# Self-attention's row-maximum product: 64 rows a head instead of 128, two heads on the two row halves of TensorE's array

## The chip, the cores and the metric

The kernel runs on one core of a Trainium2 chip. The metric is the device time of one execution in microseconds (us), the median of several runs. TensorE (PE) multiplies, VectorE (DVE), ScalarE (ACT) and GpSimd (POOL) do the element-wise work, SyncE (SP) issues the DMAs.

## What is computed

One transformer block on x (2 x 1024 rows of 256) with a context of 2 x 154 rows of 192: layer norm, self-attention, layer norm, cross-attention, layer norm, gated feed-forward, each with a residual. The part that matters here is attention with 16 heads of 64:

```python
q = (xq @ wq).reshape(B, S, N_HEADS, D_HEAD)
k = (xkv @ wk).reshape(B, T, N_HEADS, D_HEAD)
v = (xkv @ wv).reshape(B, T, N_HEADS, D_HEAD)
scale = D_HEAD ** (-0.5)
attn = jnp.einsum('bihd,bjhd->bhij', q, k) * scale
attn = jax.nn.softmax(attn, axis=-1)
out = jnp.einsum('bhij,bjhd->bihd', attn, v).reshape(B, S, D_ATTN)
return out @ wo + bo
```

## The kernel before, in words

Activations lie transposed in SBUF (features on partitions). A float32 operand of a product is held as a high half that TensorE's fp32r format keeps exactly (written by ACT) and a low half, the rest (a subtraction on DVE or POOL); a projection is then three products, high x high, high x low, low x high.

Attention goes over `NPAIR` = 16 pairs of heads (8 pairs for each of the 2 sequences), J = 0 to 15. Each engine has an order written out by hand, `SELF_ORDER` and `CROSS_ORDER` (L61, L76), which `bodies` (L151) emits once per pair as one body: words with "-" belong to pair J-1, without a sign to J, with "+" to J+1, with "++" to J+2. So a body of self-attention holds the softmax products of one pair beside the preparation of the next. The words, with PE's work for each:

- K, Q, V (two halves of 512 columns each): the projections, 6 matmuls of 512 columns at L502 each.
- T: four transposes of values (L529). M: the transpose of the row maxima (L556).
- X0 to X31: the product for the row maximum (L546). One matmul takes 128 queries against 512 keys of one head; DVE then takes its maximum over the 512 keys (`tensor_reduce`, L767). Before the change a query's operand `qq[b][:, h, ...]` holds 128 rows for each head: its 64 high halves on the head's own partitions (0-63 for head 0 of the pair, 64-127 for head 1) and its 64 low halves on the other ones; `kk` holds the high halves of the keys on both (the second copy is ACT's, semaphore `k_twice`).
- S u.h: the scores of 128 keys against 512 queries for head h, two matmuls (L569, L570), the second of which also subtracts the row maximum; ACT takes the exponential (L950).
- P u: probabilities times values, one matmul for each of the two heads, into 64 output columns each (L582), in float32: the trace has two MATMUL records for each. D: the sums of the exponentials, of the same form (L591), followed by a reciprocal on DVE (L784).
- Y half.m: the output projection, three matmuls (L606 to L608) into bank `FOLD`, then an addition on DVE (L794).

What ties the engines around X: two PSUM banks take the X products in turn (`mx_banks` = 2). X number n waits until DVE has read number n-2 (`x_read`, "`after(pe, S["x_read"], n - plan.mx_banks + 1)`"). DVE works its own order strictly one after the other, and that order is not changed:

```python
"dve": "R0- K0+ D1- K1+ Q0+ X0+ X1+ X2+ Q1+ X3+ X4+ X5+ X6+ X7+ X8+ X9+ X10+ Y0.0- X11+ X12+ X13+ R1- "
       "X14+ Y0.1- X15+ X16+ C0+ X17+ X18+ X19+ X20+ X21+ X22+ X23+ X24+ X25+ X26+ X27+ X28+ M0+ D0 "
       "X29+ X30+ Y1.0- X31+ C1+ M1+ Y1.1-",
```

There K and Q are the two subtractions that give the low halves (L761), R the multiplication by the reciprocal (L789), C a small maximum (L775), M a copy (L780).

On TensorE a matmul whose operands lie on 128 partitions and that gives 128 columns uses the whole array, which is called whole-array here; P and D use half the columns each and are called column-half here.

Of the kernel before, what the change touches and what calls it, by code (L numbers as in the profile page):

```python
# [30 lines left out]
HEADS, DH = 16, 64  # L31
# [3 lines left out]
P = 128  # L35
KD = DM // P
KC, PC = 2, DC // 2
HALF = 512
# [21 lines left out]

SELF_ORDER = {  # L61
# [102 lines left out]
def block_kernel(nc, io, out):  # L164
    with ExitStack() as ctx:
# [157 lines left out]
        def prep_use(plan, kind, a, J, b):  # L323


            use = plan.at[kind] + a
            which = (plan.nprep * b + use) % plan.prep_banks
            g = plan.nprep * J + use
            return g, PREP - which, sems[plan][f"prep_free{which}"], g if plan.prep_banks == 1 else g // 2
# [82 lines left out]
        def _(pe):  # L412
            def bank(n, width=HALF):
                return psum[:, n, 0:width]
# [75 lines left out]
            def attention(plan, h_count):  # L490
                S = sems[plan]
# [13 lines left out]
                def emit(steps, par):  # L505
                    for kind, J, a, dp in steps:
# [24 lines left out]
                            mm.then_inc(S["prep_ready"], 1)  # L531
                        elif kind == "X":
                            n = plan.tiles * J + a
                            if a == 0:
                                pe.wait_ge(S["k_twice"], plan.khalf * (J + 1))
                            if a in (0, plan.tiles // 2):
                                if plan is CROSS:
                                    pe.wait_ge(S["q_lo"], 4 * J + 2 + 2 * (a // (plan.tiles // 2)))
                                else:
                                    _, _, split, reads = prep_use(plan, "Q", a // (plan.tiles // 2), J, b)  # L540
                                    pe.wait_ge(split, reads + 1)
                            after(pe, S["x_read"], n - plan.mx_banks + 1)
                            if plan.khalf == 2:
                                half, h, t, kh = a // 16, a // 2 % 2, a // 4 % 4, a % 2
                                q0 = half * HALF + t * P
                                mm = pe.matmul(bank(PV + plan.pv_banks + a % plan.mx_banks), qq[b][:, h, q0:q0 + P], kk[b][:, h, kh * HALF:(kh + 1) * HALF],  # L546
                                               start=True, stop=True)
                            else:
                                for h in range(2):
                                    mm = pe.matmul(psum[:, PV + plan.pv_banks + a % plan.mx_banks, h * plan.keys:(h + 1) * plan.keys],  # L550
                                                   qq[b][:, h, a * P:(a + 1) * P], kk[b][:, h, 0:plan.keys], start=True, stop=True)
# [129 lines left out]
        def _(dve):  # L681
# [62 lines left out]
            def attention(plan, h_count):  # L744
# [3 lines left out]
                def emit(steps, par):  # L748
                    for kind, J, a, dp in steps:
# [13 lines left out]
                        elif kind == "X":  # L763
                            dve.wait_ge(S["x_ready"], plan.tiles * J + a + 1)
                            if plan.khalf == 2:
                                half, h, t, kh = a // 16, a // 2 % 2, a // 4 % 4, a % 2
                                dve.tensor_reduce(m_part[:, half, h, t, kh:kh + 1], psum[:, PV + plan.pv_banks + a % plan.mx_banks, :], AX.X,  # L767
                                                  ALU.max).then_inc(S["x_read"], 1)
                            else:
# [371 lines left out]
```

## Time and profile before

| | |
|---|---|
| runs of the kernel before | 1566.72, 1568.81, 1576.96 us |
| median | 1568.81 us |
| span of the profiled execution | 1578.7 us |
| PE busy | 1469.8 us (93%) |
| DVE busy | 979.5 us (62%) |
| mean granted TensorE clock | 0.958 of full speed |

The page gives the profiled execution's span and no separate time for it; it lies 9.9 us (0.6%) above the median of the runs. Self-attention fills the stretch from about 60 to 930 us. How to read the views: a busy time counts the records' own durations, and those of matmuls are modelled and overlap each other, so the pace of PE is read from the starts of successive matmuls. "PEld" is the load of the weights (the stationary operand) that goes before each matmul.

### The profile page before, as it was taken

The page shows a single profiled execution, that of the slowest core. Times are in us where ns is not written, and L with a number is a line of the kernel's source. Part 1 is how long each engine was busy: PE and PEld are TensorE (multiplying, and loading weights), DVE is VectorE, ACT ScalarE, POOL GpSimd, SP SyncE. Part 2 cuts the span into 40 slices and gives each one's busy share as a digit, 9 for nine tenths or more (in the row PEclk, how much of TensorE's full clock was granted, in tenths as well). Part 3 has the DMA queues.
Part 4 walks back from the last instruction along what each step waited for, and adds up shares of the span by engine and source line. Part 5 has one row for each costly group of instructions (what it writes and reads, how often), then busy time and mean ns, then how long its engine had stood idle before and what let it go on. Part 6 is the DMA issues. An engine that isn't in the chain of part 4 may idle for free.

```text
span 1578.7 us, 21167 instructions
## 1 busy us (share of the span) xinstructions
PE 1469.8 (93%) x5921; PEld 821.4 (52%) x5921; DVE 979.5 (62%) x1311; ACT 858.7 (54%) x1498; POOL 923.3 (58%) x513
## 2 busy tenths in 40 slices
PE   5589999999999999999999998689999999968998
PEld 3344555555555555555555543344555555426776
DVE  6457766766776676677667643536777777744333
ACT  4346565565655656565565643546666667535333
POOL 6026767757766775776677687436667777553000
PEclk9689999999999999999999998869999999979999
DMA  2000000000000000000000000200000000000000
GB/s 70 11 14 14 13 2 14 15 0 13 13 1 13 13 13 0 13 13 0 13 14 3 1 13 0 88 20 18 24 24 24 12 24 24 7 1 0 14 13 27
DMA packets 35737, 24.07 MB, mean 15 GB/s; under 512 B 2845, under 2 KB 35443, under 8 KB 35443
## 3 DMA queue, kind: packets, MB, share of 16 engines
q1 hardware_dynamic: 35699, 23.60, 4.9%
q8 instruction: 20, 0.33, 0.1%
q14 instruction: 18, 0.15, 0.0%
HBM read 21.23 MB, written 2.10 MB: 15 GB/s over the span
## 4 chain that ended last, share of the span: by engine, by line
PE 83%; ACT 6%; DVE 5%; POOL 3%; issue 2%; DMA 0%; ACTq 0%; SPq 0%; DVEq 0%; POOLq 0%
PE psum L582 20%; PE psum L502 13%; PE psum L569 11%; PE psum L546 9%; PE psum L570 8%; PE psum L655 5%; PE psum L591 4%; PE psum L644 3%; PE psum L606 2%; PE psum L608 2%; PE psum L607 2%; ACT probs L950 2%; PE psum L550 1%; PE psum L443 1%; PE psum L529 1%
## 5 line engine op out<-in xcount | busy, mean ns | idle before, releaser
L1083 POOL TENSOR_TENSOR acc<-acc,probs 128x1024 f32<-128x1024 f32 x192 | 458.2, 2386 | 184.3 <-ACT probs L950 175.1
L950 ACT ACTIVATE probs<-psum 128x512 f32<-128x512 f32 (+1 forms) x640 | 368.1, 594 | 256.9 <-PE psum L570 234.5
L767 DVE TENSOR_REDUCE m_part<-psum 128x1 f32<-128x512 f32 x512 | 344.9, 687 | 113.0 <-PE psum L546 108.7
L582 PE MATMUL psum<-probs,val 128*64 128x512 f32 (+1 forms) x1280 | 340.8, 620 | 0.2 <-ACT probs L950 0.2
L784 DVE RECIPROCAL recip<-psum 128x512 f32<-128x512 f32 x64 | 214.9, 3358 | 79.0 <-PE psum L591 79.0
L1083 POOL TENSOR_TENSOR acc<-probs 128x1024 f32<-128x1024 f32 (+1 forms) x64 | 152.7, 2386 | 120.1 <-ACT probs L950 71.0
L569 PE MATMUL psum<-qq,self_keys_hh 128*128 128x512 f32 x512 | 219.3, 428 | 2.2 <-ACT probs L950 2.1
L546 PE MATMUL psum<-self_keys_hh,qq 128*128 128x512 f32 x512 | 210.5, 431 | 6.1 <-DVE qq L761 2.8
L570 PE MATMUL psum<-qm,self_keys_lm 128*128 128x512 f32 x512 | 202.9, 396 | 0.0
L569 PEld LDWEIGHTS psum<-qq,self_keys_hh 128*128 128x128 f32 x512 | 96.7, 189 | 121.5 <-ACT probs L950 56.6
L546 PEld LDWEIGHTS psum<-self_keys_hh,qq 128*128 128x128 f32 x512 | 96.1, 190 | 117.5 <-DVE m_part L767 60.6
L502 PE MATMUL psum<-h_hi,w_hi 128*128 (+1 forms) x256 | 112.2, 438 | 21.9 <-POOL w_lo L1049 12.1
L1092 POOL TENSOR_TENSOR qq<-q_full,qq 64x512 fp32r<-64x512 f32 x64 | 81.8, 1278 | 83.4 <-ACT q_full L924 80.8
L582 PEld LDWEIGHTS psum<-probs,val 128*64 128x64 f32 (+1 forms) x1280 | 67.0, 136 | 116.9 <-issue 100.4
L794 DVE TENSOR_TENSOR xT<-xT,psum 128x512 f32 (+1 forms) x128 | 87.5, 684 | 57.6 <-PE psum L608 56.0
L1097 POOL TENSOR_TENSOR o_lo<-oT,o_hi 128x512 fp32r<-128x512 f32 x64 | 82.1, 1283 | 60.3 <-ACT o_hi L955 59.2
L502 PE MATMUL psum<-h_hi,w_lo 128*128 (+1 forms) x256 | 106.1, 414 | 0.0
L502 PE MATMUL psum<-h_lo,w_hi 128*128 (+1 forms) x256 | 105.7, 413 | 0.0
L570 PEld LDWEIGHTS psum<-qm,self_keys_lm 128*128 128x128 f32 x512 | 97.0, 189 | 13.6
L920 ACT ACTIVATE qq<-psum 64x512 fp32r<-64x512 f32 x128 | 75.6, 590 | 39.7 <-PE psum L502 38.3
L770 DVE TENSOR_REDUCE m_part<-psum 128x2 f32<-128x308 f32 x128 | 60.8, 475 | 56.1 <-PE psum L550 56.1
L955 ACT ACTIVATE o_hi<-oT 128x512 fp32r<-128x512 f32 x64 | 40.4, 632 | 93.7 <-DVE oT L789 55.6
(122 smaller groups left out, 2165.5 us busy)
## 6 DMA issues: line engine op xcount, KB each, us to landing
w_raw<-in_L_xattn_ff_w SPq DMA_DIRECT2D x3, 1024.0 KB, 6.8
x_in<-in_x SPq DMA_DIRECT2D x4, 512.0 KB, 4.2
w_raw<-in_L_xattn_sa_wq SPq DMA_DIRECT2D x16, 128.0 KB, 2.1
w_raw<-in_L_xattn_sa_wk SPq DMA_DIRECT2D x16, 128.0 KB, 2.3
w_raw<-in_L_xattn_sa_wv SPq DMA_DIRECT2D x16, 128.0 KB, 2.4
qm<-m_rows SPq DMA_DIRECT2D x128, 2.0 KB
wo_raw<-in_L_xattn_sa_wo SPq DMA_DIRECT2D x16, 128.0 KB, 2.1
w_raw<-in_L_xattn_ca_wq SPq DMA_DIRECT2D x16, 128.0 KB, 2.3
```

The source lines that it names most:

```text
L502: mm = pe.matmul(bank(prep, n), w, x, start=(k == 0 and m == 0), stop=(k == kin - 1 and m == 2))
L546: mm = pe.matmul(bank(PV + plan.pv_banks + a % plan.mx_banks), qq[b][:, h, q0:q0 + P], kk[b][:, h, kh * HALF:(kh + 1) * HALF], start=True, ...
L569: pe.matmul(psum[0:plan.ks, SC + h, :], kk[b][:, h, ks], qq[b][:, h, qs], start=True, stop=False)
L570: pe.matmul(psum[0:plan.ks, SC + h, :], kl[b][:, h, ks], qm[b][:, h, qs], start=False, stop=True).then_inc(S["s_ready"], 1)
L582: mm = pe.matmul(psum[d, PV + half % plan.pv_banks, :], val[b][0:plan.ks, kt, d], probs[a % 4][0:plan.ks, h, :], start=(kt == 0), stop=(kt ...
L767: dve.tensor_reduce(m_part[:, half, h, t, kh:kh + 1], psum[:, PV + plan.pv_banks + a % plan.mx_banks, :], AX.X, ALU.max).then_inc(S["x_rea ...
L784: dve.reciprocal(recip[:], psum[:, FOLD, :]).then_inc(S["sums_read"], 1)
L794: dve.tensor_tensor(x, x, psum[:, FOLD, :], ALU.add).then_inc(S["y_added"], 1)
L950: act.activation(probs[u % 4][0:plan.ks, h, :], psum[0:plan.ks, SC + h, :], ACT.Exp, scale=SCALE).then_inc(S["exp_done"], 1)
L1083: pool.tensor_tensor(total, last if kt == 1 else total, now, ALU.add).then_inc(S["acc_done"], 1)
L1092: pool.tensor_tensor(qq[b][other, h, half], q_full[own, a, :], qq[b][own, h, half], ALU.subtract).then_inc(S["q_lo"], 1)
L1097: pool.tensor_tensor(o_lo[:], oT[:], o_hi[:], ALU.subtract).then_inc(S["o_lo"], 1)
```

## The change

For self-attention alone the product for the row maximum contracts 64 rows, the high halves of one head on that head's own partitions, in place of 128. So the low halves of the queries no longer enter the row maximum (it is subtracted from the scores and divides out again). The index of a product is turned so that an even X and the odd one after it are head 0 and head 1 of the same queries and keys: the first lies on partitions 0-63, the second on 64-127, and they write two banks. X0 and X16 no longer wait for the second copy of the keys (`k_twice`) and for the low halves of the queries, but for their high halves (`hi_ready`). PE's order is rewritten so that the 32 X stand in 16 pairs; the order of DVE, ACT, POOL and SP stays. All lines from L541 on move down by one (L546 is L547 in the changed kernel, L582 is L583).

```diff
@@ SELF_ORDER
-    "pe": "S0.0 S0.1 K0+ P13- S1.0 P14- S1.1 D1- K1+ S2.0 S2.1 P15- P0 P1 S3.0 Q0+ S3.1 S4.0 P2 S4.1 S5.0 "
-          "X0+ Q1+ X1+ S5.1 X2+ S6.0 Y0.0- X3+ P3 X4+ V0+ X5+ X6+ P4 V1+ X7+ X8+ P5 X9+ S6.1 X10+ S7.0 "
-          "X11+ P6 X12+ T0+ X13+ S7.1 X14+ S8.0 Y0.1- S8.1 X15+ X16+ P7 X17+ S9.0 X18+ T1+ X19+ S9.1 X20+ "
-          "S10.0 X21+ S10.1 X22+ S11.0 X23+ P8 X24+ X25+ P9 X26+ S11.1 X27+ S12.0 X28+ M0+ S12.1 D0 S13.0 "
-          "S13.1 P10 X29+ P11 S14.0 X30+ S14.1 Y1.0- X31+ P12 S15.0 S15.1 Y1.1- M1+",
+    "pe": "S0.0 S0.1 K0+ P13- S1.0 P14- S1.1 D1- K1+ S2.0 S2.1 P15- P0 P1 S3.0 Q0+ S3.1 S4.0 P2 S4.1 S5.0 X0+ "
+          "X1+ Q1+ S5.1 X2+ X3+ S6.0 Y0.0- P3 X4+ X5+ V0+ X6+ X7+ P4 V1+ X8+ X9+ P5 S6.1 X10+ X11+ S7.0 P6 "
+          "X12+ X13+ T0+ S7.1 X14+ X15+ S8.0 Y0.1- S8.1 X16+ X17+ P7 S9.0 X18+ X19+ T1+ S9.1 X20+ X21+ S10.0 "
+          "S10.1 X22+ X23+ S11.0 P8 X24+ X25+ P9 X26+ X27+ S11.1 S12.0 X28+ X29+ M0+ S12.1 D0 S13.0 S13.1 P10 "
+          "P11 S14.0 X30+ X31+ S14.1 Y1.0- P12 S15.0 S15.1 Y1.1- M1+",
@@ PE, kind "X"
-                            if a == 0:
+                            if a == 0 and plan is CROSS:
                                 pe.wait_ge(S["k_twice"], plan.khalf * (J + 1))
                             if a in (0, plan.tiles // 2):
+                                second = a // (plan.tiles // 2)
                                 if plan is CROSS:
-                                    pe.wait_ge(S["q_lo"], 4 * J + 2 + 2 * (a // (plan.tiles // 2)))
+                                    pe.wait_ge(S["q_lo"], 4 * J + 2 + 2 * second)
                                 else:
-                                    _, _, split, reads = prep_use(plan, "Q", a // (plan.tiles // 2), J, b)
-                                    pe.wait_ge(split, reads + 1)
+                                    pe.wait_ge(S["hi_ready"], plan.nsplit * J + plan.khalf + second + 1)
                             after(pe, S["x_read"], n - plan.mx_banks + 1)
                             if plan.khalf == 2:
-                                half, h, t, kh = a // 16, a // 2 % 2, a // 4 % 4, a % 2
+                                half, t, kh, h = a // 16, a // 4 % 4, a // 2 % 2, a % 2
                                 q0 = half * HALF + t * P
-                                mm = pe.matmul(bank(PV + plan.pv_banks + a % plan.mx_banks), qq[b][:, h, q0:q0 + P], kk[b][:, h, kh * HALF:(kh + 1) * HALF],
-                                               start=True, stop=True)
+                                own = slice(h * DH, (h + 1) * DH)
+                                mm = pe.matmul(bank(PV + plan.pv_banks + a % plan.mx_banks), qq[b][own, h, q0:q0 + P],
+                                               kk[b][own, h, kh * HALF:(kh + 1) * HALF], start=True, stop=True)
@@ DVE, kind "X"
-                                half, h, t, kh = a // 16, a // 2 % 2, a // 4 % 4, a % 2
+                                half, t, kh, h = a // 16, a // 4 % 4, a // 2 % 2, a % 2
```

On PE, from X14 to the product P7 behind it (L546 and L547 are X, L569/L570 and L570/L571 are S, L606 to L608 and L607 to L609 are Y0.1, L582 is P). Before:

```order
L546 MATMUL psum<-self_keys_hh,qq 128x512 [waits self_x_read]
L569 MATMUL psum<-qq,self_keys_hh 128x512 [waits self_exp_done,self_m_moved1,self_q_again]
L570 MATMUL psum<-qm,self_keys_lm 128x512
L606 MATMUL psum<-o_hi,wo_hi 128x512 [waits self_y_added]
L607 MATMUL psum<-o_lo,wo_hi 128x512
L608 MATMUL psum<-o_hi,wo_lo 128x512
L569 MATMUL psum<-qq,self_keys_hh 128x512 [waits self_exp_done]
L570 MATMUL psum<-qm,self_keys_lm 128x512
L546 MATMUL psum<-self_keys_hh,qq 128x512 [waits self_x_read]
L546 MATMUL psum<-self_keys_hh,qq 128x512 [waits self_x_read,self_prep_free0]
L582 MATMUL psum<-probs,val 64x512 [waits self_exp_done]
```

The same place in the changed kernel:

```order
L547 MATMUL psum<-self_keys_hh,qq 128x512 [waits self_x_read] x2
L570 MATMUL psum<-qq,self_keys_hh 128x512 [waits self_exp_done,self_m_moved1,self_q_again]
L571 MATMUL psum<-qm,self_keys_lm 128x512
L607 MATMUL psum<-o_hi,wo_hi 128x512 [waits self_y_added]
L608 MATMUL psum<-o_lo,wo_hi 128x512
L609 MATMUL psum<-o_hi,wo_lo 128x512
L570 MATMUL psum<-qq,self_keys_hh 128x512 [waits self_exp_done]
L571 MATMUL psum<-qm,self_keys_lm 128x512
L547 MATMUL psum<-self_keys_hh,qq 128x512 [waits self_x_read,self_hi_ready]
L547 MATMUL psum<-self_keys_hh,qq 128x512 [waits self_x_read]
L583 MATMUL psum<-probs,val 64x512 [waits self_exp_done]
```

X15 has moved from behind Y0.1 to a place ahead of S8.0, beside X14; X17 has moved ahead of P7, beside X16.

The second place is PE around T1 (L529) and the scores that follow it. Before:

```order
L546 MATMUL psum<-self_keys_hh,qq 128x512 [waits self_x_read]
L529 MATMUL psum<-ident,valT 128x128 [waits self_prep_free0]
L529 MATMUL psum<-ident,valT 128x128 x3
L546 MATMUL psum<-self_keys_hh,qq 128x512 [waits self_x_read]
L569 MATMUL psum<-qq,self_keys_hh 128x512 [waits self_exp_done]
L570 MATMUL psum<-qm,self_keys_lm 128x512
L546 MATMUL psum<-self_keys_hh,qq 128x512 [waits self_x_read]
```

The same place in the changed kernel:

```order
L547 MATMUL psum<-self_keys_hh,qq 128x512 [waits self_x_read] x2
L529 MATMUL psum<-ident,valT 128x128 [waits self_prep_free0]
L529 MATMUL psum<-ident,valT 128x128 x3
L570 MATMUL psum<-qq,self_keys_hh 128x512 [waits self_exp_done]
L571 MATMUL psum<-qm,self_keys_lm 128x512
L547 MATMUL psum<-self_keys_hh,qq 128x512 [waits self_x_read] x2
```

X19 has moved ahead of T1, and X20 and X21 stand together behind S9.1.

## Rows read from the trace of the kernel before

**Rows 1.** The page: busy time of the engines, then the chain that ended last.
```profile
PE 1469.8 (93%) x5921; PEld 821.4 (52%) x5921; DVE 979.5 (62%) x1311; ACT 858.7 (54%) x1498; POOL 923.3 (58%) x513
...
PE 83%; ACT 6%; DVE 5%; POOL 3%; issue 2%; DMA 0%; ACTq 0%; SPq 0%; DVEq 0%; POOLq 0%
```

**Rows 2.** Stretch: its us; busy us PE, PEld, DVE, ACT, POOL; PEclk; DMA share, GB/s.
```profile
442.70:885.00 442.30, 442.30 (x1799) 240.62 (x1799) 302.24 (x414) 257.69 (x444) 304.56 (x144) 1.00 0.03 9
60.00:110.00 50.00, 42.03 (x116) 24.04 (x117) 27.83 (x46) 20.66 (x34) 8.43 (x4) 0.79 0.04 11
```

**Rows 3.** PE's waits from 110 to 900 us: all there are.
```profile
PE psum L569 <- ACT probs L950: 0.3, 1, 0.3
```

**Rows 4.** PE's timeline: start us, us, engine, line, operation, count.
```profile
501.02 0.39 PE L546 MATMUL psum<-self_keys_hh,qq 128*128 128x512 f32 x1
501.33 1.08 PE L582 MATMUL psum<-probs,val 128*64 128x512 f32 x4
502.34 0.50 PE L546 MATMUL psum<-self_keys_hh,qq 128*128 128x512 f32 x1
502.68 0.40 PE L502 MATMUL psum<-h_hi,w_hi 128*128 x1
502.92 0.39 PE L502 MATMUL psum<-h_lo,w_hi 128*128 x1
```

**Rows 5.** PE's timeline around three P that follow each other, and the page's group.
```profile
545.14 2.79 PE L582 MATMUL psum<-probs,val 128*64 128x512 f32 x12
547.87 0.50 PE L569 MATMUL psum<-qq,self_keys_hh 128*128 128x512 f32 x1
...
L582 PE MATMUL psum<-probs,val 128*64 128x512 f32 (+1 forms) x1280 | 340.8, 620 | 0.2 <-ACT probs L950 0.2
```

**Rows 6.** Timeline of weight loads around the one product on few rows (34).
```profile
9.41 0.19 PEld L443 LDWEIGHTS psum<-xT,mean_w 128*128 128x128 f32 x1 [0.34 <-issue]
10.36 0.14 PEld L428 LDWEIGHTS psum<-ident,vec_rows 34*128 34x128 f32 x1 [0.76 <-issue]
10.54 0.31 PEld L423 LDWEIGHTS psum<-ident,x_in 128*128 128x128 f32 x3
```

**Rows 7.** DVE's timeline: reads of X (L767) and what stands between them.
```profile
500.77 1.39 DVE L761 TENSOR_TENSOR qq<-psum,qq 64x512 fp32r<-64x512 f32 x2
502.19 1.38 DVE L767 TENSOR_REDUCE m_part<-psum 128x1 f32<-128x512 f32 x2
504.51 1.29 DVE L767 TENSOR_REDUCE m_part<-psum 128x1 f32<-128x512 f32 x2 [0.94 <-PE psum L546]
...
510.69 0.69 DVE L794 TENSOR_TENSOR xT<-xT,psum 128x512 f32 x1
511.29 2.17 DVE L767 TENSOR_REDUCE m_part<-psum 128x1 f32<-128x512 f32 x3
...
514.73 0.69 DVE L794 TENSOR_TENSOR xT<-xT,psum 128x512 f32 x1
515.33 1.28 DVE L767 TENSOR_REDUCE m_part<-psum 128x1 f32<-128x512 f32 x2
...
527.25 3.36 DVE L784 RECIPROCAL recip<-psum 128x512 f32<-128x512 f32 x1 [0.72 <-PE psum L591]
```

**Rows 8.** PE's timeline at the products that those DVE rows follow.
```profile
504.08 0.40 PE L546 MATMUL psum<-self_keys_hh,qq 128*128 128x512 f32 x1
...
511.90 0.60 PE L529 MATMUL psum<-ident,valT 128*128 128x128 f32 x4
...
512.57 0.39 PE L569 MATMUL psum<-qq,self_keys_hh 128*128 128x512 f32 x1
...
514.18 0.39 PE L608 MATMUL psum<-o_hi,wo_lo 128*128 128x512 f32 x1
...
526.12 1.08 PE L591 MATMUL psum<-acc,ones 128*64 128x512 f32 x4
```

**Rows 9.** PE's waits from 60 to 110 us.
```profile
PE psum L546 <- DVE qq L761: 2.8, 1, 2.8
```

## The prediction

> **What bounds the kernel now.** I read the page first: PE is busy for 93% of the span, no other engine for more than 62%, and the chain that ended last lies on PE for 83% [rows 1]. Then the stretches: from 442.7 to 885 us PE is busy for all of the 442.3 us at a granted clock of 1.00 (its level of 2.4 GHz), and DVE for 302 us of them [rows 2]. Last the waits: from 110 to 900 us PE waited 0.3 us in all [rows 3]. So in self-attention, outside its start, PE runs from one instruction into the next. Two things follow: what shortens PE's own stream is gained in full, and any wait that is new on PE is lost in full. DVE has slack on average, but it reads X products in a fixed order between other work.
>
> **How PE spends its time.** A whole-array matmul of 512 columns starts 0.23 to 0.24 us after the one before it [rows 4]; I take 0.233. P is a change of shape: three P in a row last from 545.14 to 547.87, 2.73 us, one alone from 501.33 to 502.34, 1.01 us, so each further P costs 0.86 and 0.15 is paid once [rows 4, 5]. The start of P comes 0.31 after the whole-array matmul ahead of it, 0.08 to 0.10 late, and the second whole-array matmul behind P 0.34 after the first, 0.11 late [rows 4]. I read that as a pause of 0.10 at each change of shape, and behind it a weight load that lies in the open: 0.05 for 64 columns, 0.11 for 128. In the pure stream the load is hidden under the matmul before. That prices an entrance into P at 0.15 and one into a shape with 128 columns at 0.21.
>
> Is the new product, 64 rows by 128 columns, a change of shape too? There is one near case, a product on 34 rows. The load ahead of the whole-array stream there is 0.76 us idle with no releaser, starts at 10.36 after that stream has finished and does not run ahead beneath it, and so does the load of the next whole-array product at 10.54 [rows 6]. I take it as a change of shape, both ways.
>
> The Trainium skill says the same against this change: by "TensorEngine Tiling (Array Packing)", Key Properties, another tiling mode, though not another tile of one mode, drains TensorE. By the same page's table of theoretical speedup a contraction of 64 rows or less gains up to 2x. Which wins is what the sum below decides; by the second sentence alone the X would be worth half their time, and that is the fourth rival.
>
> **The X products themselves.** 32 X of 0.233 are 7.46 us in a body. If the two of a pair run side by side, as the two heads of P do (1280 records of 620 ns would be 794 us, and P is busy for 340.8 [rows 5]), 16 pairs of 0.22 are 3.52. Saved: 3.94.
>
> **The changes of shape.** Counted in the two orders of PE. Before, a body has 16 column-half stretches (P15 P0 P1 together, D0 and D1 among them), with 16 entrances to whole-array. After, P10 and P11 stand together, so 15; the 16 pairs of X are stretches of their own; 8 borders lie directly between a pair and a P (at P3, P4, P5, P6, P7, two sides of X24 X25, and P9 to X26), which leaves 15 + 16 - 8 = 23 returns to whole-array. Added: 16 entrances into row halves at 0.21, 3.36; 7 more returns at 0.21, 1.47; one entrance into P less, -0.15. Together 4.68. Against the 3.94 saved the stream itself is 0.74 us longer in a body.
>
> The bounds of this unseen price: if it is nothing, the stream is 3.94 + 0.35 (the excursion into P that the joining of P10 and P11 saves) = 4.3 shorter. If the pairs do not run side by side at all, each costs a further 0.22, 3.5 in a body. I take the middle value, the price of P, the row it is nearest to.
>
> **The new waits.** X n waits for the read of X n-2. Singles left time for that; now the second of a pair needs the second of the pair ahead. DVE starts 0.44 after the X starts (504.08, 504.51), a second read comes 0.60 later, each lasts 0.69 [rows 7, 8]. A pair that starts at 0 is read until 0.44 + 0.60 + 0.69 = 1.73. Then the load in the open, 0.11, and about 0.05 for the semaphore: the next pair's second product can't start before 1.89. On PE the next pair starts at 0.22 + 0.21 + work between + 0.21, with S = 0.46, Y = 0.69, P = 0.86, and T = 0.67 - 0.23 = 0.44 (511.90 to 512.57 less one X) [rows 8]. Where a P lies between, an entrance of 0.15 and a further 0.21 come in. Most gaps suffice. Six do not:
>
> X3 to X5: DVE has Q1's two subtractions before X3 (from 500.77 to 502.19, 1.42 [rows 7]), so X3 is read until 0.44 + 0.72 + 1.42 + 0.69 = 3.27, restart at 3.43; PE comes after 0.22 + 0.21 + S + Y + 0.15 + P + 0.21 = 2.80. Wait 0.63.
>
> X11 to X13: DVE adds Y0.0 before X11 (0.60, 510.69 to 511.29), restart at 2.49; PE comes at 0.22 + 0.21 + S + 0.15 + P + 0.21 = 2.11. Wait 0.38.
>
> X15 to X17: DVE adds Y0.1 before X15, and Y0.1 now comes after X15 on PE, not before. Its last matmul starts 0.22 + 0.21 + 2 x 0.46 = 1.35 after the pair, the addition 0.55 later (514.18, 514.73), the read 0.60 later, 0.69 long: 3.19, restart 3.35. PE comes at 0.43 + S + Y + S + 0.21 = 2.25. Wait 1.10, the largest.
>
> X19 to X21, across T1 and one S: 1.54 against 1.89. Wait 0.35. X25 to X27, across P9: 1.44 against 1.89. Wait 0.45.
>
> X29 to X31: X29 stands behind D0's reciprocal on DVE. D0 starts on PE 1.02 after the pair (0.43, M 0.03, S, a pause of 0.10), the reciprocal 1.13 later (526.12, 527.25), 3.36 long, the read 0.69: 6.20, restart 6.36. PE, by way of D0, two S, P10, P11 and one S, comes at 5.83. Wait 0.53.
>
> The gaps across two S (X22, X28) come to 1.56, but there the pair ahead started its first product early by its own wait, so the reads have ended in time. The six are 3.44 us in a body. Nothing behind PE covers this: it had no waits to give back [rows 3].
>
> **What costs nothing.** The turned index changes only which maximum goes where. The waits of X0 and X16 for `k_twice` and the low halves go; PE waited once, 2.8 us, for the latter, at the start [rows 9], but DVE makes those low halves before it reads X0 in its unchanged order, so the read is no earlier. The later reads of X31 and X15 feed C1 and C0, with several P and S between them and M.
>
> **The sum.** 0.74 + 3.44 = 4.2 us in a body, in the 15 bodies that prepare a next pair beside softmax work; the first pair's X lie in the opening stretch, where PE is busy for 42 of 50 us and goes by DVE's reads [rows 2], and change nothing. 15 x 4.2 = 63 us. On the profiled execution's span of 1578.7 that is 1642, on the median of the runs, 9.9 lower, 1568.8 + 63 = 1632. From no change 1% can be told, 16 us. I forecast 1632, with 1605 to 1660 if the mechanism holds (a quarter off in the waits is 13 us, 0.05 off in the 22 added borders 16).
>
> **Rivals.**
> Pairs one after the other: the second product has a wait of its own, which P's second has not, and that may keep it apart. Then 16 x 0.22 more, less what hides in the six waits (6 x 0.22): 2.2 x 15 = 33, 1665. Against it: P's heads overlap as the busy time says [rows 5]. Chance 0.10.
>
> Borders cost nothing, waits as above: for it only that the 34-row case is one row. The stream is 4.3 shorter, but the gaps shrink with it: the six waits grow by 0.2 to 0.4 each, to some 5.1. 0.8 x 15 = 12, 1581. Chance 0.15.
>
> Borders cost as with P, but the waits are hidden, because reads come earlier than my rows say: 0.74 x 15 = 11, 1580. Chance 0.06.
>
> Faster: borders cost nothing and DVE keeps pace with half the waits gone (2.5 a body): 4.3 - 2.5 = 1.8 x 15 = 27, 1542, and with all of them gone 1504. It is decided where the waits in a body stay under the 4.3 us that the stream saves. For it: DVE's load is 68% in this stretch; against it: the read of a pair takes 1.29, and the order puts an addition and a reciprocal inside a pair. Chance 0.11.
>
> **How the numbers follow.** The forecast holds 0.58, the slower rival 0.10, the two near no change 0.21, the faster one 0.11. The two near no change lie just inside 1% (to 1584.5), but some of their spread falls outside: same 0.17, faster 0.12, slower 0.71. The range runs from 1572, which takes in the two, to 1668, which takes in the serial pairs; the faster case is left out.
>
> **What would show it.** In the changed trace: L547 records in pairs with starts a few ns apart; the load of the next whole-array product 0.1 after them and not beneath them; PE waiting for DVE's L768 six times in a body, longest ahead of X17; PE's busy share in the stretch below 100%; a body longer by some 4 us. Wrong would be: pairs of 0.22 between whole-array products at the plain pace (then the border price falls), starts 0.22 apart (then they are serial), or PE's waits for L768 under 1 us in a body.

## The result and the profile after

| | before | after |
|---|---|---|
| median of 4 runs each | 1570.01 us | 1643.30 us |
| all runs | 1566.72 to 1576.96 | 1641.12 to 1644.03 |
| span of the profiled execution | 1578.7 | 1641.7 |

The ratio is 1.0447, with a 95% interval from 1.0409 to 1.0484: slower by 4.5%. (Here and below the ratio is an estimate from the single runs, so it is not exactly the quotient of the medians beside it.) Forecast were 1632 us in a range from 1572 to 1668. By the spans of the two profiled executions the change costs 63.0 us, by the medians 73. The other ten I put down to a stretch behind self-attention, in which the granted clock of one and the same kernel differs from run to run (last section).

The page of the changed kernel. PE is as busy by share as in [rows 1], and DVE, which was 5% of the chain, is 7%:

```profile
PE 1522.3 (93%) x5921; PEld 787.3 (48%) x5921; DVE 970.4 (59%) x1311; ACT 855.9 (52%) x1498; POOL 922.9 (56%) x513
...
PE 81%; DVE 7%; ACT 6%; issue 3%; POOL 3%; DMA 0%; ACTq 0%; SPq 0%; DVEq 0%; POOLq 0%
...
L547 PE MATMUL psum<-self_keys_hh,qq 64*128 64x512 f32 x512 | 178.3, 511 | 18.0 <-DVE m_part L768 14.9
```

The same stretch as in [rows 2] (columns as there) has fallen from 100% busy to 98.9%, and does fewer matmuls, 1682 for 1799. That is 6.5% less work, of which the busy share shows 1.1 points:

```profile
442.70:885.00 442.30, 437.25 (x1682) 208.05 (x1680) 276.54 (x380) 240.80 (x419) 283.20 (x134) 1.00 0.03 10
```

**A pair between whole-array products.** PE's timeline of the changed kernel (start us, us, engine, line, operation, count). L571 is the second half of an S, L570 the first of the next:

```profile
541.02 0.40 PE L571 MATMUL psum<-qm,self_keys_lm 128*128 128x512 f32 x1
541.35 0.49 PE L547 MATMUL psum<-self_keys_hh,qq 64*128 64x512 f32 x2
541.78 0.50 PE L570 MATMUL psum<-qq,self_keys_hh 128*128 128x512 f32 x1
542.11 0.40 PE L571 MATMUL psum<-qm,self_keys_lm 128*128 128x512 f32 x1
542.44 1.08 PE L583 MATMUL psum<-probs,val 128*64 128x512 f32 x4
```

The two products of a pair are merged in one row of 0.49 us, no longer than one of them: they run side by side, as the change intends. But the row starts 0.33 after the one before (0.23 is the plain pace), the next whole-array product starts 0.43 after it, and the one after that 0.33 later again. From 541.02 to 542.11 are 1.09 us for a pair and two starts of the plain pace (0.47): the pair costs 0.62. Two whole-array X cost 0.47. So the product itself is halved, and still the pair costs 0.15 more than the two products that it replaces. The forecast had 0.64 for it (0.21 + 0.22 + 0.21).

The weight loads show where that goes. Within a whole-array stretch the record of a load starts 0.23 us ahead of its matmul (the median), beneath the matmul before. From 200 to 880 us of the changed kernel there are 613 changes of shape of all kinds, 89 of them between X and P, and at every one the load starts within 3 ns of its matmul: none runs ahead.

**A pair held back.** The same view at X16, X17, behind Y0.1 (L607 to L609):

```profile
546.90 0.40 PE L609 MATMUL psum<-o_hi,wo_lo 128*128 128x512 f32 x1
547.13 0.40 PE L570 MATMUL psum<-qq,self_keys_hh 128*128 128x512 f32 x1
547.37 0.40 PE L571 MATMUL psum<-qm,self_keys_lm 128*128 128x512 f32 x1
547.70 0.49 PE L547 MATMUL psum<-self_keys_hh,qq 64*128 64x512 f32 x1
548.79 0.50 PE L547 MATMUL psum<-self_keys_hh,qq 64*128 64x512 f32 x1 [0.60 <-DVE m_part L768]
```

and DVE at that time (L768 reads an X, L795 adds a Y):

```profile
545.97 0.69 DVE L768 TENSOR_REDUCE m_part<-psum 128x1 f32<-128x512 f32 x1
547.45 0.69 DVE L795 TENSOR_TENSOR xT<-xT,psum 128x512 f32 x1 [0.79 <-PE psum L609]
548.06 1.28 DVE L768 TENSOR_REDUCE m_part<-psum 128x1 f32<-128x512 f32 x2
```

X14 is read at 545.97. X15, its partner, is in its bank as well, but stands behind the addition of Y0.1 in DVE's order; DVE sits idle for 0.79 us until PE has made Y0.1, adds, and reads X15 from 548.06 to 548.75. X17 starts at 548.79. It comes 1.09 us after X16, where the forecast had 1.10. The row says "0.60" idle: the record of X16 is modelled to last until 548.19, so a wait on PE is read from the starts, not from the idle column. The list of PE's waits, which had a single line in [rows 3], shows only 8.6 us from 110 to 950 us for the same reason:

```profile
PE psum L547 <- DVE m_part L768: 8.6, 14, 0.8
```

From the starts, the second product of a pair comes late at six places in every steady body, and at no other: 0.61 at X5, 0.50 at X13, 1.10 at X17, 0.38 at X21, 0.43 at X27, 0.42 at X31 (medians over the 15 bodies), 3.44 us in all. In the other ten pairs it starts within 10 ns of the first.

**The length of a body.** The steady part repeats so evenly that one number carries most comparisons below: the time from the first X of one body to that of the next, taken as the mean over 13 bodies (J = 2 to J = 15, counted from 0). Before it is 55.66 us (X0 of J = 2 at 163.2, of J = 15 at 886.9), after 59.62 (170.6, 945.7). The difference is 3.96.

### The profile page after: what moved, and what is told of

It is laid out like the page before. It is cut to its first block, busy times and chain, and to the rows that moved or that the text cites. A ratio compares the mean times of both kernels' runs of the same rounds, so it can differ in the third digit from the quotient of the medians.

```text
span 1641.7 us, 21178 instructions
## 1 busy us (share of the span) xinstructions
PE 1522.3 (93%) x5921; PEld 787.3 (48%) x5921; DVE 970.4 (59%) x1311; ACT 855.9 (52%) x1498; POOL 922.9 (56%) x513
## 4 chain that ended last, share of the span: by engine, by line
PE 81%; DVE 7%; ACT 6%; issue 3%; POOL 3%; DMA 0%; ACTq 0%; SPq 0%; DVEq 0%; POOLq 0%
PE psum L583 18%; PE psum L502 13%; PE psum L570 11%; PE psum L547 9%; PE psum L571 8%; PE psum L656 5%; PE psum L592 4%; PE psum L645 2%; PE psum L607 2%; DVE m_part L768 2%; ACT probs L951 2%; PE psum L609 2%; PE psum L608 2%; DVE qq L762 1%; PE psum L529 1%
## 5 line engine op out<-in xcount | busy, mean ns | idle before, releaser
L768 DVE TENSOR_REDUCE m_part<-psum 128x1 f32<-128x512 f32 x512 | 335.8, 686 | 167.3 <-PE psum L547 163.4
L583 PE MATMUL psum<-probs,val 128*64 128x512 f32 (+1 forms) x1280 | 337.4, 619 | 0.2 <-ACT probs L951 0.2
L570 PE MATMUL psum<-qq,self_keys_hh 128*128 128x512 f32 x512 | 235.9, 461 | 2.3 <-ACT probs L951 2.3
L571 PE MATMUL psum<-qm,self_keys_lm 128*128 128x512 f32 x512 | 203.1, 397 | 0.0
L547 PE MATMUL psum<-self_keys_hh,qq 64*128 64x512 f32 x512 | 178.3, 511 | 18.0 <-DVE m_part L768 14.9
L570 PEld LDWEIGHTS psum<-qq,self_keys_hh 128*128 128x128 f32 x512 | 97.2, 190 | 162.2 <-issue 77.7
L547 PEld LDWEIGHTS psum<-self_keys_hh,qq 64*128 64x128 f32 x512 | 67.6, 188 | 167.8 <-DVE m_part L768 113.2
L502 PE MATMUL psum<-h_hi,w_hi 128*128 (+1 forms) x256 | 115.6, 452 | 20.3 <-POOL w_lo L1050 10.9
L795 DVE TENSOR_TENSOR xT<-xT,psum 128x512 f32 (+1 forms) x128 | 87.6, 684 | 76.1 <-PE psum L609 75.6
L583 PEld LDWEIGHTS psum<-probs,val 128*64 128x64 f32 (+1 forms) x1280 | 68.2, 136 | 114.7 <-issue 91.4
L571 PEld LDWEIGHTS psum<-qm,self_keys_lm 128*128 128x128 f32 x512 | 97.4, 190 | 7.8
```

The lines of the kernel that those rows point to most:

```text
L502: mm = pe.matmul(bank(prep, n), w, x, start=(k == 0 and m == 0), stop=(k == kin - 1 and m == 2))
L570: pe.matmul(psum[0:plan.ks, SC + h, :], kk[b][:, h, ks], qq[b][:, h, qs], start=True, stop=False)
L571: pe.matmul(psum[0:plan.ks, SC + h, :], kl[b][:, h, ks], qm[b][:, h, qs], start=False, stop=True).then_inc(S["s_ready"], 1)
L583: mm = pe.matmul(psum[d, PV + half % plan.pv_banks, :], val[b][0:plan.ks, kt, d], probs[a % 4][0:plan.ks, h, :], start=(kt == 0), stop=(kt ...
L795: dve.tensor_tensor(x, x, psum[:, FOLD, :], ALU.add).then_inc(S["y_added"], 1)
```

## The experiments

Ten kernels ran. In the times below "before" stands for the kernel before on the same chip and in the same session; its median was 1579.64 (e1 to e4), 1577.99 (e5 to e8) and 1577.48 us (e9, e10), with single runs from 1566.45 to 1581.04. Body lengths come from each kernel's own trace.

| kernel | median us | ratio to before (95%) | body us |
|---|---|---|---|
| before | 1570.01 | | 55.66 |
| after | 1643.30 | 1.0447 (1.0409 to 1.0484) | 59.62 |
| e1 order only | 1614.17 | 1.0227 (1.0161 to 1.0292) | 58.05 |
| e2 rows only | 1680.51 | 1.0668 (1.0607 to 1.0730) | 62.33 |
| e3 spaced | 1593.28 | 1.0086 (1.0056 to 1.0117) | 56.50 |
| e4 joined | 1596.45 | 1.0107 (1.0042 to 1.0173) | 56.71 |
| e5 one exchange on DVE | 1616.05 | 1.0239 (1.0222 to 1.0256) | 58.53 |
| e6 old waits of X0, X16 | 1636.19 | 1.0361 (1.0338 to 1.0384) | 59.62 |
| e7 both on one half | 1659.69 | 1.0506 (1.0465 to 1.0548) | 61.10 |
| e8 joined, second try | 1554.41 | 0.9861 (0.9835 to 0.9888) | 54.36 |
| e9 64 rows beside P only | 1557.27 | 0.9869 (0.9830 to 0.9909) | 54.22 |
| e10 joined, one more | 1551.95 | 0.9850 (0.9816 to 0.9883) | 54.15 |

**e1, the order alone.** The changed kernel with these edits:

```diff
-                            if a == 0 and plan is CROSS:
+                            if a == 0:
...
-                                    pe.wait_ge(S["hi_ready"], plan.nsplit * J + plan.khalf + second + 1)
+                                    _, _, split, reads = prep_use(plan, "Q", second, J, b)
+                                    pe.wait_ge(split, reads + 1)
...
-                                mm = pe.matmul(..., qq[b][own, h, q0:q0 + P], kk[b][own, h, ...])
+                                mm = pe.matmul(..., qq[b][:, h, q0:q0 + P], kk[b][:, h, ...])
```

> The changed order of TensorE with the old product on 128 rows and the old waits of X0 and X16 (the index with two heads side by side stays). Leaves out nothing. Theory (the change costs by borders between shapes and by waits for reads, each about half): the borders fall to 15 into and 15 out of the column-half shape, 0.36 us a body fewer than before; the waits stay, but each gap is 0.25 us longer because an X pair takes 0.47 in place of 0.22: about 2.8 us a body, the largest ahead of X17. Net 2.4 x 15 = 37 us over before, about 1607. Rival 1 (only the 64-row shape costs): 1565, no wait of TensorE for the reads. Rival 2 (only the order costs): 1643.

Measured: 1614.17 us, a body of 58.05, 2.39 over before where 2.4 was expected. PE waits in the trace, longest ahead of X17 again (the second X comes 1.20 after the first, where 0.23 is plain). So with the product on 128 rows untouched, pairing it in the order costs 36 us by bodies (15 x 2.39), 34.5 by medians. Rival 1 falls, and so does rival 2: the order by itself costs a good half of what the change costs, and not all of it.

**e2, the shape alone.** The changed kernel with the "pe" line of the kernel before.

> The 64-row product, two heads by turns, in the old order of TensorE, where most X stand alone. Theory: 28 stretches in the row-half shape in each body, each with an entrance and a return; 28 x 0.21 + 12 x 0.21 = 8.4 us a body of borders more than before, 0.4 saved where two X stand together and by the plain length, no new waits for reads: 8.0 x 15 = 120 us over before, about 1690. Rival 1 (a border costs nothing, only the order's waits do): 1570. Rival 2 (borders at half the price): 1630.

Measured: 1680.51 us, 101 above before; a body of 62.33, 6.67 longer, where 8.0 was expected. The only wait of PE that the list shows from 110 to 900 us is the 0.3 us of [rows 3], the starts show no late X either, and in the stretch PE is busy throughout:

```profile
442.70:885.00 442.30, 442.30 (x1603) 204.17 (x1602) 271.38 (x372) 229.70 (x397) 270.18 (x128) 1.00 0.03 8
```

So the borders alone, with no wait at all, cost more than the whole change. That a border is free falls; at half price the time would have been 1630. The expectation took too little for what the new product saves: X5 X6, X7 X8, X15 X16 and X24 X25 start within 10 ns of each other here too, so 28 stretches of 0.22 stand in place of 32 products of 0.233, which saves 1.3 in a body and not 0.4. Forty borders were added in a body, 28 entrances and 12 returns: (6.67 + 1.3) / 40 is 0.20 for each, close to the 0.21.

e1 and e2 don't add up to the change (2.39 + 6.67 against 3.96), because pairing does two things: it makes the waits, and it cuts the added borders from 40 to 22 and lets all the products run two at a time.

**e3, the waits taken out.** The changed kernel with these orders (ACT, POOL and SP as before):

```diff
-          "... S7.1 X14+ X15+ S8.0 Y0.1- S8.1 X16+ X17+ P7 S9.0 X18+ X19+ T1+ S9.1 X20+ X21+ S10.0 "
-          "S10.1 X22+ X23+ S11.0 P8 X24+ X25+ P9 X26+ X27+ S11.1 S12.0 X28+ X29+ M0+ S12.1 D0 S13.0 S13.1 P10 "
-          "P11 S14.0 X30+ X31+ S14.1 Y1.0- P12 ..."
+          "... S7.1 S8.0 X14+ X15+ Y0.1- S8.1 X16+ X17+ P7 S9.0 X18+ X19+ T1+ S9.1 S10.0 X20+ X21+ "
+          "S10.1 S11.0 X22+ X23+ P8 S11.1 X24+ X25+ P9 S12.0 X26+ X27+ M0+ S12.1 D0 X28+ X29+ S13.0 S13.1 "
+          "P10 P11 S14.0 S14.1 Y1.0- X30+ X31+ P12 ..."
-    "dve": "... X2+ Q1+ X3+ X4+ X5+ X6+ ... X10+ Y0.0- X11+ ... X14+ Y0.1- X15+ ... X28+ M0+ D0 X29+ X30+ Y1.0- X31+ ..."
+    "dve": "... X2+ X3+ Q1+ X4+ X5+ Y0.0- X6+ ... X10+ X11+ ... X14+ X15+ Y0.1- ... M0+ D0 X28+ X29+ Y1.0- X30+ X31+ ..."
```

> The changed kernel with the orders of TensorE and VectorE laid out so that both X of a pair are read one after the other with nothing between (Q1, the additions of Y0.0, Y0.1, Y1.0 and the reciprocal of D0 stand between pairs), and at least 1.9 us of other work from pair to pair. Theory: the 3.5 us of waits a body fall to under 0.5, one border fewer (0.2): 3.2 x 15 = 48 us below the changed kernel, about 1595, 25 above before. Rival 1 (borders are the whole cost and the waits are covered elsewhere): 1640. Rival 2 (VectorE's new order delays the low halves and TensorE waits there): above 1610.

Measured: 1593.28 us, 50 below the changed kernel and 14 above before; a body of 56.50, 3.12 shorter, where 3.2 was expected. Of the six late partners five are on time and X17 is late by 0.09; X23, which was not among them, now comes 0.30 late. Both are short enough for the records to cover them. The waits from 110 to 900 us are single ones, and the stretch is full again:

```profile
PE psum L502 <- DVE qq L762: 0.7, 1, 0.7
PE psum L570 <- ACT probs L951: 0.3, 1, 0.3
PE psum L547 <- DVE m_part L768: 0.2, 1, 0.2
...
442.70:885.00 442.30, 442.25 (x1771) 213.41 (x1768) 290.46 (x413) 249.00 (x437) 301.32 (x143) 1.00 0.03 9
```

This also answers what the new product is worth at its best: the kernel on 64 rows is still 0.84 us a body behind the one on 128, 0.39 of it in the two waits and 0.45 in borders that the halved products don't pay for.

**e4, a first try at fewer borders.** If a visit to another shape costs 0.35 us, the kernel before pays it 16 times in a body for P and D. e4 joins P13 P14 P15 D1, P4 P5, P8 P9 and P10 P11 in the order of PE, on the kernel before:

```diff
-    "pe": "S0.0 S0.1 K0+ P13- S1.0 P14- S1.1 D1- K1+ S2.0 S2.1 P15- P0 P1 ... X5+ X6+ P4 V1+ X7+ X8+ P5 ... P8 X24+ X25+ P9 ... P10 X29+ P11 ..."
+    "pe": "S0.0 S0.1 K0+ S1.0 S1.1 P13- P14- P15- D1- K1+ S2.0 S2.1 P0 P1 ... X5+ X6+ P4 P5 V1+ X7+ S6.1 X8+ ... P8 P9 X24+ X25+ ... P10 P11 X29+ ..."
```

> The kernel before, with the product on 128 rows, whose order joins column-half products (P13 P14 P15 D1, P4 P5, P8 P9, P10 P11) so that a body has 11 stretches of that shape in place of 16. Theory (a visit to another shape costs 0.35 us whatever it holds): 5 x 0.35 x 15.5 = 27 us below before, about 1543, if the rest is as well covered; waits of up to 0.4 a body may come in. Rival 1 (it is P itself, not its border, that costs the 0.35): 1570. Rival 2 (joined P leave the exponentials or the reads behind, and TensorE waits): 1560 to 1590.

Measured: 1596.45 us, a body of 56.71, 1.05 longer. A miss, by rival 2: PE waits for exponentials, which it did once for 0.3 us before [rows 3]:

```profile
PE psum L582 <- ACT probs L950: 10.2, 14, 0.7
PE psum L569 <- ACT probs L950: 9.6, 29, 0.4
```

It also lies above the 1560 to 1590 of that rival. My reading, from the orders: the join put V1 behind P5, and ACT copies V1 ahead of S6.0's exponential, so S7.0 and the P behind it had to wait. The trace bears this out: ACT sits idle for 2.84 us until PE has made V1, copies it from 515.58, takes the exponential from 516.07 to 516.66, and S7.0 starts at 516.72, 0.65 after the X ahead of it. Likewise, by the orders, K1's copies stand ahead of S2.0's exponential, and S3.0 starts 0.48 late. e8 changes both places, and moves X and DVE's additions besides.

**e5, one exchange.** The changed kernel with two words of DVE's order exchanged:

```diff
-           "X14+ Y0.1- X15+ X16+ C0+ ..."
+           "X14+ X15+ Y0.1- X16+ C0+ ..."
```

> The changed kernel with two neighbours of VectorE's order exchanged: X15 is read before the addition of Y0.1, not after it. Theory (X17's wait of 1.10 us a body exists because that addition, which waits for TensorE, stands between the reads of one pair): the wait ahead of X17 goes, the others stay, body 59.63 to 58.5, 15 x 1.1 = 16 us below the changed kernel, about 1627. Rival (the wait only moves to a neighbour): 1640 to 1643.

Measured: 1616.05 us, 27 below the changed kernel by medians; a body of 58.53, 1.09 shorter, which times 15 is 16.4, and X17 starts within 10 ns of X16. The other five places keep their waits to 0.02. The rival falls. The 11 us that the medians give beyond 16 are not this wait. The profiled executions differ by 1641.7 - 1621.0 = 20.7, of which 15.3 lie in the 15 bodies, 2.3 ahead of the second pair's X0 (113.8 and 111.5) and 3.1 behind self-attention.

**e6, the old waits of X0 and X16.** The first two edits of e1's diff, with the slices of 64 rows.

> The changed kernel with the old waits of X0 and X16 put back (second copy of the keys, low halves of the queries). Theory: the waits were met anyway in the steady bodies, which stay at 59.63 us; in the opening X0 starts some 2.6 us later again, and the product then gets the low halves behind it sooner or not at all: total within 5 us of the changed kernel (1638 to 1645). Rival (the dropped waits were worth something): 1650 or more.

Measured: 1636.19 us, a little under the expected range, with bodies of 59.62, unchanged. X0 of the first pair moves from 57.8 to 60.5, but X0 of the last pair is where it was (945.7 and 945.0). So the dropped waits bring nothing. The medians differ by 7, the spans by 3.9, of which 0.7 arises in self-attention.

**e7, both products on one half of the rows.** On the changed kernel, the same line on PE and on DVE:

```diff
-                                half, t, kh, h = a // 16, a // 4 % 4, a // 2 % 2, a % 2
+                                half, h, t, kh = a // 16, a // 2 % 2, a // 4 % 4, a % 2
```

> The changed kernel with the old index, in which the two products of a pair belong to one head and so lie on the same half of the rows. Nothing is left out. Theory (the pair costs 0.22 because two row halves work side by side; on one half the second must come 0.22 later): 0.22 x 16 a body more, less what hides in the six waits, 2.2 x 15 = 33 us above the changed kernel, about 1676; starts within a pair 0.22 apart. Rival (products of 64 rows are quick by themselves, or run one after the other in both kernels): 1643.

Measured: 1659.69 us, half way between theory and rival, and a body of 61.10, 1.47 longer where 2.2 was expected. A pair without a wait, in PE's timeline of e7:

```profile
541.96 0.40 PE L571 MATMUL psum<-qm,self_keys_lm 128*128 128x512 f32 x1
542.28 0.73 PE L547 MATMUL psum<-self_keys_hh,qq 64*128 64x512 f32 x2
542.94 0.50 PE L502 MATMUL psum<-h_hi,w_hi 128*128 x1
```

The pair's row is 0.73 us long against 0.49 and the next product starts 0.66 after it against 0.43: on one half the two run one after the other, which takes 0.23 more. (The second starts 0.34 after the first, not 0.22 as expected, and the product behind it 0.32 after the second, not 0.43.) So the side-by-side running is worth what was counted for it; in the body more of it than I allowed is hidden, since a pair that itself takes 0.23 more gives DVE that time: beyond that plain 0.34 the late partners shrink to 0.1 or less at all but X17.

**e8, joined again with ACT and DVE brought along.** On the kernel before:

```diff
+    "pe": "S0.0 S0.1 K0+ S1.0 S1.1 P13- P14- D1- K1+ S2.0 S2.1 P15- P0 P1 S3.0 Q0+ S3.1 S4.0 P2 S4.1 S5.0 X0+ Q1+ X1+ "
+          "S5.1 X2+ S6.0 Y0.0- X3+ P3 X4+ V0+ X5+ S6.1 X6+ V1+ X7+ P4 P5 X8+ X9+ S7.0 T0+ X10+ P6 X11+ X12+ S7.1 S8.0 "
+          "X13+ Y0.1- X14+ S8.1 X15+ P7 X16+ X17+ S9.0 T1+ X18+ S9.1 X19+ S10.0 X20+ S10.1 X21+ S11.0 X22+ P8 P9 X23+ "
+          "X24+ S11.1 S12.0 X25+ S12.1 X26+ M0+ D0 X27+ X28+ S13.0 S13.1 P10 P11 S14.0 X29+ S14.1 X30+ Y1.0- X31+ P12 ..."
-    "dve": "... X6+ X7+ X8+ X9+ X10+ Y0.0- ... R1- X14+ Y0.1- X15+ ... X28+ M0+ D0 X29+ X30+ Y1.0- X31+ ..."
+    "dve": "... X6+ Y0.0- X7+ X8+ X9+ X10+ ... R1- X14+ X15+ Y0.1- ... X26+ M0+ D0 X27+ X28+ X29+ X30+ Y1.0- X31+ ..."
-    "act": "... Q1+ V0+ S5.1 V1+ S6.0 B0+ ..."
+    "act": "... Q1+ S5.1 V0+ S6.0 V1+ B0+ ..."
```

> The kernel before (128 rows) with joined column-half products, second try: P13 P14 D1, P15 P0 P1, P4 P5, P8 P9, P10 P11, so 11 stretches in place of 16, X spaced by at least 0.7 us or set behind a P, ScalarE taking S5.1 and S6.0 ahead of the two value copies, VectorE's additions moved between. The first try lost more to waits for exponentials (the trace shows 20 us of them from 110 to 900 us) than its borders gave. Theory: 5 x 0.35 = 1.75 us a body off with waits under 0.4: body 54.1 to 54.4, 19 to 24 us below before. Rival (joined P always leave ScalarE's exponentials late): body 55.7 or more.

Measured: 1554.41 us, a ratio of 0.9861 (0.9835 to 0.9888), a body of 54.36, 1.30 shorter, at the edge of what was expected. The stretch is full, with more matmuls in it than [rows 2] has (1843 for 1799):

```profile
442.70:885.00 442.30, 442.30 (x1843) 252.26 (x1839) 308.46 (x425) 264.57 (x457) 310.35 (x146) 1.00 0.03 9
```

The price of a border holds in the other direction too: five visits fewer, with the product unchanged, gain 1.30 of the 1.75 that they are worth. The rest I put down to small delays, of up to 0.15 each, at places where X or an exponential is now just late (X10, X25, S14.0).

**e9, 64 rows where only one border is added.** On e8:

```diff
-                                half, h, t, kh = a // 16, a // 2 % 2, a // 4 % 4, a % 2
+                                half, t, kh, h = a // 16, a // 4 % 4, a // 2 % 2, a % 2
...
+                                own = slice(h * DH, (h + 1) * DH) if a in (8, 9, 11, 12, 16, 17, 23, 24, 27, 28) else slice(0, P)
```

(The index is turned on PE and on DVE, so that the two of a pair lie on different halves.)

> The kernel of e8 with 64 rows for only the five pairs of X that stand directly behind a column-half product (X8 X9, X11 X12, X16 X17, X23 X24, X27 X28), and 128 for the rest; those five leave the low halves of the queries out of the row maximum. Theory (each border has its price, so beside a P a pair needs one entrance more, 0.21, and saves 0.25): 0.04 x 5 = 0.2 us a body, 3 us in all, at or just below e8, 1548 to 1555. Rival (the row halves' gain comes out where only one border is added): 1.25 a body, 19 us below e8, about 1535.

Measured: 1557.27 us, above the expected 1548 to 1555, but the body is as expected: 54.22, 0.14 below e8 where 0.20 was forecast. The medians, from different sessions, can't tell the two apart. The rival's 1.25 a body is excluded. Even beside a P the halved product is worth next to nothing.

**e10, one more join** (P6 P7, with the X behind them moved one place, DVE's order to match, and ACT's T0 and S7.1 ahead of the second B).

> The kernel of e8 with P6 and P7 joined too (10 stretches of column-half products in a body), the X behind them moved one place, and on ScalarE T0 and S7.1 ahead of the queries' second copy. Theory: 0.35 us a body less if no wait comes in, 5 us below e8, about 1549. Rival (the bodies are now tight enough that a further join is paid back in waits): 1554 or more.

Measured: 1551.95 us, a ratio of 0.9850 (0.9816 to 0.9883), a body of 54.15, 0.22 shorter than e8, where 0.35 was expected. Its interval overlaps that of e8, so by time the two are equal; both beat both kernels.

## Why the prediction was right

**PE as the bound.** Held. What was added to PE's stream came out in full, 3.96 us in each steady body. The 15 bodies that were priced account for 58.0 of the 63.0 us between the spans: the first 2.8 (there is no Y of an earlier pair yet, and X17 is not late), thirteen of 3.96, and the last 3.7, up to the last S of self-attention.

**The pair side by side.** Held. One row of 0.49 us for two products, and e7 shows what it would be otherwise, 0.73.

**The price of the borders.** Held, very slightly dear. Forecast 0.64 for a pair between whole-array products, measured 0.62. For the stream, 0.74 a body was forecast; the body without its waits is 3.96 - 3.44 = 0.52 longer, and e3, which has one return fewer (0.53 by the same sum), is 0.45 above before without its waits. For the 22 added borders (3.94 + 0.52) / 22 is 0.20 each, as e2 gives it too, against 0.21. That 64 rows are a change of shape was right, though the row that it was read from [rows 6] was thin ground: the idle 0.76 us stand ahead of the 34-row product's own load, and the whole-array load at 9.41 has 0.34 of idle time ahead of it with no change of shape at all. The loads above show it well, at every border. This agrees with the rule that I cited from the Trainium skill, "TensorEngine Tiling (Array Packing)", Key Properties, that another mode drains TensorE. The speedup of up to 2x in the Trainium skill, "TensorEngine Tiling (Array Packing)", Theoretical Speedup, is borne out by the product alone (0.49 us for two), and not by the kernel.

**The new waits.** Held, place by place:

| | X5 | X13 | X17 | X21 | X27 | X31 | sum |
|---|---|---|---|---|---|---|---|
| forecast | 0.63 | 0.38 | 1.10 | 0.35 | 0.45 | 0.53 | 3.44 |
| measured | 0.61 | 0.50 | 1.10 | 0.38 | 0.43 | 0.42 | 3.44 |

The sum is exact by luck (X13 too small, X31 too large); the places are not. The order by size is right but for X13 and X31, which change places. A second piece of luck is inside each: the load in the open, 0.11, was put behind the read, and it stands ahead of it. Where DVE waits for an X of the new shape, its read starts 0.53 after it, where 0.44 was taken, and the late X starts 0.05 after the read that it waits for has ended, at all six places, where 0.16 was taken. e5 removed the largest wait with one exchange, e3 all but 0.09 of the six, and each gave back about what it was worth. e1 has waits of the same kind without the new shape, at X5, X13, X17, X21 and X31, and at X29 in place of X27.

One sign of being wrong that the prediction named was PE's waits for L768 under 1 us in a body. In the list of waits that is so: 8.6 us over some 14 bodies. The sign was badly chosen, since the modelled records cover most of each wait; by the starts it is 3.44.

**What costs nothing.** Held for the dropped waits (e6).

**The sum.** 63 us were forecast, and the spans say 63.0, but that is luck: two errors cancel in it. A body was put at 4.18 and measured 3.96, which makes 5 us less over the 15. And the opening, where I had put nothing, cost 4.6: from the first X0 to the second the changed kernel takes 56.0 us, the one before 48.8, and only 2.6 of these 7.2 come back by X0's earlier start. The median came out at 1643 and not 1632 because I took 9.9 us off the span to get from the profiled execution to the median; of all steps this one failed. In every run that lists both, the time lies about 1.8 us above the span, so the profiled execution of the kernel before took about 1580.5 us and was none of the three whose median, 1568.8, I started from. In the later sessions the same kernel's median was 1577.48 to 1579.64, and against those the change costs 64 to 66 us.

**The rivals.** Serial pairs: refuted by the row of 0.49. Borders free: refuted by e2. Waits hidden: refuted by the starts and e5. Faster: it needed free borders and half of the waits gone, and had neither.

## What to carry to other kernels

A product that uses half of the array and runs two at a time saves half of its streaming, here 0.25 us a pair, but each change between any two of the three shapes here costs 0.15 to 0.2 us; so count the changes in PE's order before the products, and put like shapes next to each other. In this kernel, whose PE never waits, that alone was worth 1.4% (e8), without touching a single product.

Two engines that hand buffers to each other, each in a fixed order, deserve a walk on paper: with two buffers, the second of a pair waits for the second of the last pair, and whatever the reading engine has between those two reads, above all something that waits for PE itself, lands on PE. When PE's order is changed, DVE's and ACT's belong to the change.

## What the runs showed that I had not expected

**The clock behind self-attention moves the whole by some 10 us.** The same kernel's runs spread by that much: before from 1566.83 to 1581.04 beside e1 to e4, e3 from 1581.31 to 1596.11. The clock tells where. In the first 120 us behind self-attention (the layer norm and the start of cross-attention) it is 0.74 in the profiled execution before and the same after, and 0.84 in that of e3, whose span of 1582.1 is 11 below its median:

```profile
965.00:1085.00 120.00, 90.83 (x285) 46.28 (x285) 56.17 (x68) 57.48 (x100) 55.16 (x40) 0.74 0.11 37
```

```profile
979.00:1099.00 120.00, 93.55 (x344) 51.16 (x342) 65.06 (x82) 66.12 (x117) 62.73 (x46) 0.84 0.12 41
```

(The first row is of the kernel before, the second of e3; the clock is the third number from the end.) In the same 120 us e3 gets through 344 matmuls, before through 285. From the last S of self-attention to the end of the program the kernel before takes 613.6 us, the changed one 614.0, and e3 602.3. At the 33rd row-maximum product of cross-attention e3 is 13.0 us ahead of the kernel before (94.8 us after that S against 107.8), at the end 11.3. In e3 the clock stays at 1.00 for over 300 us from 78 us after that S on, in the kernel before from 106 on. The clock goes between 1.2 and 2.4 GHz in this stretch, where PE waits often, and which level it has when the products resume differs from run to run. The runs that have no trace point the same way: beside e9 and e10, two runs of the kernel before took 1566.5 us at a mean granted clock of 0.970 and 0.968, and one took 1579.9 at 0.957. So of the 73 us between the medians 63 are from self-attention and its opening, and I put the rest down to this stretch; for the four runs behind the 1570.01 no clock is on record, so that part is argued and not shown. That the profiled execution lay 9.9 us above the median was nothing that a change carries along. What decides the clock there was not tried.

**The opening lost time too.** From 60 to 110 us the clock fell from 0.79 [rows 2] to 0.60, and PE's busy time from 42.03 to 40.55:

```profile
60.00:110.00 50.00, 40.55 (x95) 21.49 (x95) 25.09 (x41) 17.27 (x28) 5.12 (x3) 0.60 0.04 11
```

The first pair's X lie here in a stretch where PE goes by DVE's reads; halved products make PE no faster there, and the projections between them ran at the lower clock for longer. I had written that this stretch changes nothing. The second pair's X0 starts at 109.2 before, at 109.2 in e1 (the new order, whole-array products, a clock of 0.86), at 111.1 in e2 (the new shape, the old order, 0.67) and at 113.8 after (both, 0.60). So the order alone loses nothing there, the shape alone 1.9 us, and the two together 4.6. That the lower clock follows from less work per product was not tried by itself.
